# Causal attention with the rotary partner rows fetched by transfers, a new order of the shared expert's batches, and 71 routed blocks

## The chip, the cores and the metric

One NeuronCore of one Trainium2 chip runs the whole program as one launch. The metric is the device time in microseconds (us); lower is better. PE is the tensor engine, DVE the vector engine, ACT the scalar engine, POOL the GpSimd engine, and SP the engine that only issues transfers (ACT and POOL issue some too).

## What is computed

x has shape (8, 512, 512). A gated layer of biased cross-attention comes first, then a gated block of causal attention with rotary embeddings and a mixture of experts:

```python
x = x + tanh(g_xattn[0]) * xattn(layernorm(x), ctx, ctx, ...)      # 16 heads of 32
x = x + tanh(g_ffn[0])   * ffn(layernorm(x), ...)
# ffn(h):
def _rope(xh):                       # rotates pairs of the last 32 of each head's 64
    x0, x1 = xr[..., 0], xr[..., 1]
    rot = stack([x0 * cos - x1 * sin, x0 * sin + x1 * cos], -1)
h = h + attention(rmsnorm(h, w_ln1))         # causal, 16 heads, keys from a latent of 64
xn = rmsnorm(h, w_ln2)
logits = xn @ Wgate + expert_bias            # 8 experts, each token takes 2
h = h + shared_expert(xn) + sum over its 2 experts e of p_e * expert_e(xn)
# an expert: (silu(xn @ Wg) * (xn @ Wu)) @ Wd, inner size 256
```

There are 4096 tokens, so 8192 pairs of a token and an expert.

## The kernel before

The program has three passes, each written out as one instruction list per engine. **Pass A** (to about 900 us of the span) is the cross-attention, batch by batch. **Pass B** (`pass_b`, L790, about 850 to 1765 us) is the causal attention. **Pass C** (`pass_c`) is the rest: the shared expert and the routing of all 8 batches (about 1767 to 1992 us), then the routed experts (to the end).

In pass B each batch is 64 steps. In a step PE makes one unit of scores (L1537 to L1539), which ACT turns into exponentials (L1284), and one unit for the row maxima (L1554, L1555), which DVE reduces (L1412). Score and maximum units have two PSUM banks each: PE may not write a bank before its reader of two units ago is done. Between the units PE does "jobs" of the next batch: HT transposes the input, LAT makes the key latent, QN, QR the plain and the rotary rows of the queries for each of 4 head groups, K and V keys and values, SP the spread of the sums, O the output product, M a transpose of maxima. A table `plan` (L898) gives each job its steps and its bank; the reader of a job's bank comes one step after the job's last step (`evict`, on ACT at L1222 and on DVE at L1335), and `free` (L1437) makes PE wait for it before the bank's next job.

The rotary part goes in "turns": one for the keys ("k", from LAT) and one for each head group (from QR), 5 in a batch, 40 in all. For a turn DVE multiplies the PSUM rows by the cosines into `rc` (L1349); ACT and DVE split them into two float16 parts `qu_hi`, `qu_lo` (L1248, L1361); PE multiplies both by a matrix `swp` that swaps the rows in pairs with a sign (jobs KSW and QSW, L1480 and L1481); DVE multiplies the result by the sines into `rs` (L1368). Two steps after the job POOL adds `rs` to `rc` (L1174), then ACT and POOL split the sum into `qr_hi`, `qr_lo` (L1260, L1177), and SP stores these rows and loads them back into the stacks that the units read.

In pass C the shared expert works on batch b while batch b + 1 is made ready. PE does `up` (48 products of 512 columns), `turn` (transposes of batch b + 1), `route` (48 products of 8 columns), `down` (24 of 512) and `rank`. ACT has in this order for batch b: `normalise(b+1)`, `squash(b,0)` (L1996), two `high(b+1)` (L1961), `hidden_high(b,0)` (L2002), two `scale_gate`, `squash(b,1)`, two more `high`, `hidden_high(b,1)`, two `scale_gate`, `square(b+2)` (L1969), `exponential(b+1)`, `weights(b+1)`. `square(b+2)` reads the batch that SP loads into `z[:, (b+2) % 3]`, the buffer of batch b - 1. SP issues that load (L1786) once POOL's `add_to_output(b-1)` (L1849), which adds 1 MB of finished rows to the output in HBM, has landed; and that waits for DVE's `finish_rows` of batch b - 1 (L2260). POOL's list of batch b is `add_to_output(b-1)`, the record copies, the scatters of records into a table (L1872, 8 indirect transfers per batch), two `low_part` (L1853) and `rms(b+2)` (L1843, L1845).

The routed experts take `NB` = 72 blocks of 128 rows in a pipeline (`over`, L1765: 4 blocks written out, 16 turns of a loop of 4, and the last 4 with the drain written out).

```python
                sp.wait_ge(out_stored[b % 3], 16 * (b // 3))     # load_z, b >= 3
            act.wait_ge(z_loaded[b % 3], ...)                    # square
            act.wait_ge(up_done, 4 * b + 2 * i + 1)              # squash
```

## Time and profile before

| | |
|---|---|
| device time, 3 runs | median 2361.26 us (2359.19 to 2361.65) |
| the profiled execution's own time | 2359.61 us |
| its span in the trace | 2357.6 us |
| mean granted clock of PE | 0.963 |
| PE busy | 2130.3 us, 90% of the span |
| DVE, ACT, POOL busy | 64%, 50%, 58% |

The span is what the engines' records cover; the device time lies 2.0 us above it. Busy PE is not PE at its peak, since products overlap. A row of the timeline has the start in us, the duration in us, the engine, the line, the operation, out<-in, the shapes, how many were merged, and in brackets the engine's idle time before it and what ended it. "SPq" and "ACTq" are transfers as their engine's sequencer issues them. The clock column is the granted clock of PE as a share of 2.4 GHz; 0.50 is 1.2 GHz.

### The profile page before, as it was taken

The page shows a single profiled execution, that of the slowest core. Times are in us where ns is not written, and L with a number is a line of the kernel's source. Part 1 is how long each engine was busy: PE and PEld are TensorE (multiplying, and loading weights), DVE is VectorE, ACT ScalarE, POOL GpSimd, SP SyncE. Part 2 cuts the span into 40 slices and gives each one's busy share as a digit, 9 for nine tenths or more (in the row PEclk, how much of TensorE's full clock was granted, in tenths as well). Part 3 has the DMA queues.
Part 4 walks back from the last instruction along what each step waited for, and adds up shares of the span by engine and source line. Part 5 has one row for each costly group of instructions (what it writes and reads, how often), then busy time and mean ns, then how long its engine had stood idle before and what let it go on. Part 6 is the DMA issues. An engine that isn't in the chain of part 4 may idle for free. (4 is left out here: it accounts for less than half of the span.)

```text
span 2357.6 us, 43584 instructions
## 1 busy us (share of the span) xinstructions
PE 2130.3 (90%) x12672; PEld 972.2 (41%) x12673; DVE 1505.5 (64%) x4218; ACT 1177.9 (50%) x2316; POOL 1364.2 (58%) x1452
## 2 busy tenths in 40 slices
PE   3899999999999968899999999999976787999997
PEld 1333333333333313444444444444433343455554
DVE  3688888888888873656656656565535587344443
ACT  3355555555555543354545445454436473455553
POOL 3267767767767764265656565565451664455554
PEclk7999999999999978999999999999997898999999
DMA  5413323232332233453434435353314675666665
GB/s 172 156 56 107 95 90 108 77 113 70 107 104 76 85 101 94 139 151 95 141 119 134 129 96 161 89 155 120 102 50 118 132 179 106 110 112 113 115 108 88
DMA packets 222851, 263.78 MB, mean 112 GB/s; under 512 B 39192, under 2 KB 165004, under 8 KB 222388
## 3 DMA queue, kind: packets, MB, share of 16 engines
q1 hardware_dynamic: 197612, 212.79, 30.2%
q0 software_dynamic: 22976, 48.38, 11.9%
q8 instruction: 92, 1.51, 0.3%
q14 instruction: 99, 0.81, 0.1%
q10 hardware_dynamic: 2072, 0.28, 0.1%
HBM read 162.12 MB, written 86.80 MB: 106 GB/s over the span
## 5 line engine op out<-in xcount | busy, mean ns | idle before, releaser
L501 ACT ACTIVATE a_pt<-a_bank 128x512 f32<-128x512 f32 x512 | 305.6, 597 | 371.5 <-DVE a_bank L608 368.3
L1412 DVE CUSTOM_DVE_ANT_0 b_bank<-b_bank,b_tri 128x256 f32<-128x256 f32 (+3 forms) x512 | 253.6, 497 | 302.9 <-PE b_bank L1555 298.6
L619 DVE CUSTOM_DVE_ANT_0 a_bank<-a_bank,a_strip 128x512 f32<-128x512 f32 x512 | 353.1, 690 | 4.9 <-PE a_bank L762 4.3
L411 POOL TENSOR_TENSOR a_acc<-a_acc,a_pt 128x512 f32<-128x512 f32 x256 | 317.4, 1270 | 16.2 <-ACT a_pt L501 15.7
L1193 POOL TENSOR_TENSOR b_acc<-b_acc,b_pt 128x256 f32<-128x256 f32 (+2 forms) x384 | 270.9, 725 | 90.6 <-ACT b_pt L1284 71.3
L608 DVE TENSOR_TENSOR a_bank<-a_bank,a_band 128x256 f32<-128x256 f32 (+1 forms) x512 | 205.6, 402 | 129.6 <-PE a_bank L749 128.4
L1284 ACT ACTIVATE b_pt<-b_bank 128x256 f32<-128x256 f32 (+2 forms) x384 | 143.8, 383 | 190.9 <-PE b_bank L1539 181.0
L749 PE MATMUL a_bank<-a_q_stack,a_k_stack 128*128 128x512 f16 x512 | 199.3, 390 | 22.7 <-ACT a_pt L501 14.0
L762 PE MATMUL a_bank<-a_k_stack,a_q_stack 97*128 97x512 f16 x512 | 196.4, 384 | 4.6 <-DVE a_low L619 4.5
L1933 POOL DMA_INDIRECT out_dram<-c_z,c_to_row x72 | 114.1, 1585 | 138.7 <-DMA out_dram<-c_z,c_to_row 101.8
L408 POOL TENSOR_TENSOR a_acc<-a_pt 128x512 f32<-128x512 f32 x128 | 159.9, 1270 | 4.9 <-ACT a_pt L501 4.9
L1554 PE MATMUL b_bank<-b_k_stack,b_q_stack 96*128 96x256 f16 (+3 forms) x512 | 153.7, 300 | 9.3 <-DVE b_low L1412 5.6
L1537 PE MATMUL b_bank<-b_q_stack,b_k_stack 96*128 96x256 f16 (+3 forms) x512 | 155.5, 304 | 5.8 <-ACT b_pt L1284 4.7
L429 POOL TENSOR_TENSOR a_o_un<-a_o_un,a_den 128x512 f32<-128x512 f32 x32 | 40.8, 1276 | 204.4 <-DVE a_den L572 204.4
L1208 POOL TENSOR_TENSOR b_o_un<-b_o_un,b_den 128x512 f32<-128x512 f32 x32 | 40.7, 1273 | 196.4 <-DVE b_den L1378 191.0
L1539 PE MATMUL b_bank<-b_q_stack,b_k_stack 97*128 97x256 f16 (+3 forms) x512 | 153.4, 300 | 0.0
L1555 PE MATMUL b_bank<-b_k_stack,b_q_stack 96*128 96x256 f16 (+3 forms) x512 | 152.3, 298 | 0.0
L777 PE MATMUL a_bank<-a_pt,a_v 128*32 128x512 f32 x1024 | 142.3, 629 | 1.1 <-ACT a_pt L501 1.1
L1284 ACT ACTIVATE b_acc<-b_bank 128x512 f32<-128x512 f32 x128 | 76.4, 597 | 104.7 <-PE b_bank L1539 104.7
L749 PEld LDWEIGHTS a_bank<-a_q_stack,a_k_stack 128*128 128x128 f16 x512 | 49.5, 97 | 182.8 <-ACT a_pt L501 89.3
L1538 PE MATMUL b_bank<-b_hidden,b_far 128*128 128x128 bf16 x512 | 112.8, 220 | 0.0
L2313 DVE TENSOR_TENSOR c_xt_lo<-c_bank,c_xt_hi 128x512 f16<-128x512 f32 x72 | 49.7, 691 | 97.7 <-ACT c_xt_hi L2052 96.4
(346 smaller groups left out, 5432.3 us busy)
## 6 DMA issues: line engine op xcount, KB each, us to landing
b_q_stack<-qk_rows SPq DMA_DIRECT2D x192, 128.0 KB, 2.6
a_q_stack<-qk_rows SPq DMA_DIRECT2D x96, 128.0 KB
a_k_stack<-qk_rows SPq DMA_DIRECT2D x96, 128.0 KB
b_k_stack<-qk_rows SPq DMA_DIRECT2D x96, 128.0 KB, 2.6
a_sums<-in_x SPq DMA_DIRECT2D x34, 256.0 KB, 3.1
qk_rows<-a_qk_hi SPq DMA_DIRECT2D x64, 128.0 KB, 1.7
qk_rows<-a_qk_lo SPq DMA_DIRECT2D x64, 128.0 KB, 1.8
out_dram<-a_sums SPq DMA_DIRECT2D x32, 256.0 KB, 2.0
```

The source lines that it names most:

```text
L408: nc.gpsimd.tensor_tensor(acc[:, hh, :], pt[:, (n - HG) % SLOTS, :], mine, ALU.add).then_inc(pooled, 1)
L411: nc.gpsimd.tensor_tensor(acc[:, hh, :], acc[:, hh, :], mine, ALU.add).then_inc(pooled, 1)
L501: nc.scalar.activation(pt[:, n % SLOTS, :], st_bank[n % 2][:], ACT.Exp).then_inc(exped, 1)
L608: nc.vector.tensor_tensor(st_bank[n % 2][:, c0:c1], st_bank[n % 2][:, c0:c1], band[:, h, at:at + c1 - c0], ALU.add).then_inc(biased, 1)
L619: nc.vector.tensor_tensor_reduce(out=max_bank[step % 2][:], in0=max_bank[step % 2][:], in1=strip[:, g * HG + hh, at:at + S], scale=-1.0, s ...
L749: mm(st_bank[n % 2][:], k_stack[:, h, j * P:(j + 1) * P], q_stack[:, h, :], start=True, stop=True).then_inc(scored, 1)
L762: mm(max_bank[step % 2][:], q_stack[0:MASK + 1, h, i * P:(i + 1) * P], k_stack[0:MASK + 1, h, :], start=True, stop=True).then_inc(maxed, 1)
L1193: nc.gpsimd.tensor_tensor(sums_of, sums_of, probs(n), ALU.add).then_inc(pooled, 1)
L1284: nc.scalar.activation(probs(n), st_bank[n % 2][:, 0:w], ACT.Exp).then_inc(exped, 1)
L1412: nc.vector.tensor_tensor_reduce(out=max_bank[step % 2][:, 0:w], in0=max_bank[step % 2][:, 0:w], in1=tri[:, at:at + w], scale=-1.0, scalar ...
L1537: mm(o, k_stack[0][0:LOW, h, j * P:(j + 1) * P], q_stack[0][0:LOW, h, j * P:], start=True, stop=False)
L1554: mm(o, q_stack[0][0:LOW, h, c], k_stack[0][0:LOW, h, 0:w], start=True, stop=False)
```

## The change

Pass B: the jobs KSW and QSW, `swp` and the float16 parts of the unrotated rows are gone. ACT copies the whole float32 rows to `qu` (for the keys a further copy of 32 rows) and issues two transfers from SBUF to SBUF for each turn, one for the even and one for the odd rows, into `rs`. DVE multiplies `rs` by the sines in place, one step ahead of POOL's sum (`times_sine`); its `qu_lo` operation is gone. The signs went into the table of sines, and the turns keep their steps. Pass C: the shared expert's lists have a new order on every engine, `down` is cut in halves, records have three buffers in place of two and are scattered up to a batch later. `NB` is 71, with 15 turns of the loop and the last 7 blocks with the drain written out.

```diff
-NB = 2 * TT + E
+NB = 2 * TT + E - 1
...
-        turn_step = {r: pieces[(KSW, 0) if r == "k" else (QSW, r)][0] + 2 for r in turns["steady"]}
+        turn_step = {G3: 12, "k": 28, 0: 37, 1: 48, 2: 60}
...
+            def swap_pairs(kind, b, r, begin, end):
+                done = turns_upto(kind, b, r) - 1
+                if done:
+                    act.wait_ge(rot_sum, done)
+                for i in range(2):
+                    act.dma_start(rs[begin + i:end:2, :], qu[begin + 1 - i:end:2, :]).then_inc(swapped, 16)
...
+                if m == QR:
+                    act.wait_ge(hi_done, upto(kind, b, job, is_split))
+                    swap_pairs(kind, b, n, 0, P)
...
+            def times_sine(kind, b, r):
...
+                dve.wait_ge(swapped, 32 * turns_upto(kind, b, r))
+                nc.vector.tensor_tensor(rs[part, :], rs[part, :], rot[part, table, :], ALU.mult).then_inc(rot_sin, 1)
...
-                elif m in (KSW, QSW):
-                    src_job, hi, lo = ((LAT, 0), lat_hi, lat_lo) if m == KSW else ((QR, n), qu_hi, qu_lo)
-                    pe.wait_ge(left_dve, upto(kind, b, src_job, by_dve))
-                    pe.nop(nofuse=True)
-                    mm(o[:], swp[:], hi[:], start=True, stop=False)
-                    last = mm(o[:], swp[:], lo[:], start=False, stop=True)
...
                 if b > 1:
-                    scatter(b, (0,))
+                    scatter_some(b, 2)
                 low_part(b, 0)
-                if b == 1:
-                    scatter(0, (0, 1))
-                elif b:
-                    scatter(b, (1, 2))
-                low_part(b, 1)
-                if b == 1:
-                    scatter(0, (2, 3))
-                elif b:
-                    scatter(b, (3,))
+                if b > 1:
+                    scatter_some(b, 1)
                 if b + 2 < B:
                     rms(b + 2)
-                if b == 1:
-                    scatter(1, range(NT))
+                low_part(b, 1)
+                if b:
+                    scatter_some(b, 2 if b > 1 else NT)
...
                 squash(b, 0)
                 if more:
                     high(b + 1, 0)
                     high(b + 1, 1)
+                    scale_gate(b + 1, range(0, 2))
+                    high(b + 1, 2)
+                    high(b + 1, 3)
                 hidden_high(b, 0)
-                if more:
-                    scale_gate(b + 1, range(0, 2))
+                if b + 2 < B:
+                    square(b + 2)
                 squash(b, 1)
                 if more:
-                    high(b + 1, 2)
-                    high(b + 1, 3)
+                    scale_gate(b + 1, range(2, 4))
                 hidden_high(b, 1)
-                if more:
-                    scale_gate(b + 1, range(2, 4))
                 if b + 2 < B:
-                    square(b + 2)
+                    normalise(b + 2)
...
-            def down(b, t):
-                pe.wait_ge(h_lo_done, NI * b + NI)
+            def down(b, t, halves):
...
-                for t in range(NT):
-                    down(b, t)
+                for t in range(NT - 1):
+                    down(b, t, (0,))
+                for t in range(NT - 1):
+                    down(b, t, (1,))
+                down(b, NT - 1, (0, 1))
```

PE's list of a batch becomes: up, turns 0 and 1, up, turns 2 and 3, up, up, route, the halves of down. DVE's becomes: shares and places, low 0 and 1, activate 0, low 2 and 3, the up weights, activate 1, choose, the down weights, finish_rows; in the last batch `lay_blocks` comes after activate 0 and no longer right ahead of finish_rows.

**ACT in pass C**, the middle of batch 3. `c_th` is `squash`, `c_xt_hi` is `high`, `c_h_hi` is `hidden_high`, `c_xn,c_squares` is `square`. Before:

```order
1565 L1996 ACTIVATE c_th<-c_bank 128x512 [waits c_half_done,c_up_done]
1566 L1961 ACTIVATE c_xt_hi<-c_bank 128x4x128 [waits c_logits_done,c_up_done,c_turned] x2
1567 L2002 ACTIVATE c_h_hi<-c_hid 128x512 [waits c_downed,c_hidden]
1568 L1979 ACTIVATE c_z<-c_z,c_gate 128x512 [waits c_xn_ready]
1569 L1979 ACTIVATE c_z<-c_z,c_gate 128x512
1570 L1996 ACTIVATE c_th<-c_bank 128x512 [waits c_half_done,c_up_done]
1571 L1961 ACTIVATE c_xt_hi<-c_bank 128x4x128 [waits c_logits_done,c_up_done,c_turned] x2
1572 L2002 ACTIVATE c_h_hi<-c_hid 128x512 [waits c_downed,c_hidden]
1573 L1979 ACTIVATE c_z<-c_z,c_gate 128x512 [waits c_xn_ready]
1574 L1979 ACTIVATE c_z<-c_z,c_gate 128x512
1575 L1969 ACTIVATE c_xn,c_squares<-c_z 128x512 [waits c_turned,c_z_loaded1]
1576 L1969 ACTIVATE c_xn,c_squares<-c_z 128x512 x3
```

Of the change, the same stretch:

```order
1671 L2026 ACTIVATE c_th<-c_bank 128x512 [waits c_half_done,c_up_done]
1672 L1991 ACTIVATE c_xt_hi<-c_bank 128x4x128 [waits c_logits_done,c_up_done,c_turned] x2
1673 L2009 ACTIVATE c_z<-c_z,c_gate 128x512 [waits c_xn_ready]
1674 L2009 ACTIVATE c_z<-c_z,c_gate 128x512
1675 L1991 ACTIVATE c_xt_hi<-c_bank 128x4x128 [waits c_logits_done,c_up_done,c_turned] x2
1676 L2032 ACTIVATE c_h_hi<-c_hid 128x512 [waits c_downed,c_hidden]
1677 L1999 ACTIVATE c_xn,c_squares<-c_z 128x512 [waits c_turned,c_z_loaded2]
1678 L1999 ACTIVATE c_xn,c_squares<-c_z 128x512 x3
1679 L2026 ACTIVATE c_th<-c_bank 128x512 [waits c_half_done,c_up_done]
```

The squares of batch b + 2, which wait for its load, stood behind everything that ACT does for batch b; now the second `c_th` of batch b stands behind them.

**POOL in pass C**, one batch. `table` are the scatters, `c_h_lo` is `low_part`, `c_mean` and `c_rstd` are `rms(b+2)`. Before:

```order
765 L1849 DMA out_dram<-c_z 128x4x512 [waits c_out_done]
766 L1859 COPY c_record<-c_tok 128x8x2 [waits a_o_hi_done]
767 L1861 COPY c_record<-c_rstd 128x8
768 L1872 DMA table<-c_record,c_place_i 33792x4 [waits c_recorded,c_weighed]
769 L1872 DMA table<-c_record,c_place_i 33792x4
770 L1853 TENSOR_TENSOR c_h_lo<-c_hid,c_h_hi 128x512 [waits c_h_hi_done]
771 L1872 DMA table<-c_record,c_place_i 33792x4 [waits c_recorded,c_weighed]
772 L1872 DMA table<-c_record,c_place_i 33792x4 x3
773 L1853 TENSOR_TENSOR c_h_lo<-c_hid,c_h_hi 128x512 [waits c_h_hi_done]
774 L1872 DMA table<-c_record,c_place_i 33792x4 [waits c_recorded,c_weighed]
775 L1872 DMA table<-c_record,c_place_i 33792x4
776 L1843 TENSOR_SCALAR c_mean<-c_squares 128x4 [waits c_squared]
```

Of the change:

```order
773 L1877 DMA out_dram<-c_z 128x4x512 [waits c_out_done]
774 L1887 COPY c_record<-c_tok 128x8x2 [waits a_summed]
775 L1889 COPY c_record<-c_rstd 128x8
776 L1900 DMA table<-c_record,c_place_i 33792x4 x4
777 L1881 TENSOR_TENSOR c_h_lo<-c_hid,c_h_hi 128x512 [waits c_h_hi_done]
778 L1900 DMA table<-c_record,c_place_i 33792x4 [waits a_normed,a_o_hi_done]
779 L1900 DMA table<-c_record,c_place_i 33792x4
780 L1871 TENSOR_SCALAR c_mean<-c_squares 128x4 [waits c_squared]
781 L1873 TENSOR_TENSOR c_rstd<-c_mean,c_power 128x4 [waits c_rstd_done]
782 L1881 TENSOR_TENSOR c_h_lo<-c_hid,c_h_hi 128x512 [waits c_h_hi_done]
783 L1900 DMA table<-c_record,c_place_i 33792x4 x4
784 L1877 DMA out_dram<-c_z 128x4x512 [waits c_out_done]
```

The scatters are now 10 in a batch, and `c_mean`, which needs the squares, moved ahead of the second `c_h_lo`.

**ACT in pass B**, a turn of head group 0 of the change (before, `b_qu_hi` stood in the place of `b_qu`, with no transfer behind it):

```order
925 L1305 ACTIVATE b_pt<-b_bank 128x256 [waits b_pooled,b_scored]
926 L1263 ACTIVATE b_qu<-b_bank 128x512 [waits b_swapped,b_job_done]
927 L1232 DMA b_rs<-b_qu 64x512 [waits b_rot_sum,b_hi_done]
928 L1232 DMA b_rs<-b_qu 64x512
929 L1305 ACTIVATE b_pt<-b_bank 128x256 [waits b_pooled,b_scored]
```

The next exponential stands behind both transfers.

## Rows read from the trace of the kernel before

**Rows 1.** Windows: window, length, busy us (instructions) of each engine, clock, DMA share, GB/s.
```profile
1040.00:1680.00 640.00, 625.04 (x4361) 309.94 (x4360) 387.04 (x1130) 322.54 (x698) 365.35 (x477) 1.00 0.42 125
...
1792.00:1992.00 200.00, 165.62 (x1104) 84.06 (x1104) 143.69 (x447) 112.87 (x214) 106.47 (x115) 0.90 0.62 128
```
**Rows 2.** Timeline of PE: a swap job's first product, and the scores behind it.
```profile
1377.59 0.38 PE L1480 MATMUL b_bank<-b_qu_hi,b_swp 128*128 128x512 f16 x1
...
1378.02 0.33 PE L1537 MATMUL b_bank<-b_q_stack,b_k_stack 96*128 96x384 f16 x1
```
**Rows 3.** Who waited for whom, 980 to 1700 us: us in total, times, longest.
```profile
PE b_bank L1453 <- DVE b_qu_lo L1361: 8.9, 7, 1.3
```
**Rows 4.** Transfers of pass B: count, KB each, us to landing; and one that ACT issues.
```profile
b_k_stack<-b_kr_hi SPq DMA_DIRECT2D x56, 128.0 KB, 2.4
...
1316.39 0.52 ACTq L1288 DMA_DIRECT2D b_q_stack<-b_m_row  x1
```
**Rows 5.** Timeline at the turns of head groups 1 and 2, ACT, PE and DVE.
```profile
1332.43 0.60 ACT L1248 ACTIVATE b_qu_hi<-b_bank 128x512 f16<-128x512 f32 x1 [0.38 <-PE b_bank L1455]
...
1336.90 0.69 DVE L1368 TENSOR_TENSOR b_rs<-b_bank,b_rot 128x512 f32<-128x512 f32 x1
...
1350.44 0.60 ACT L1284 ACTIVATE b_acc<-b_bank 128x512 f32<-128x512 f32 x1
...
1351.93 0.32 PE L1537 MATMUL b_bank<-b_q_stack,b_k_stack 96*128 96x384 f16 x1
```
**Rows 6.** Chain of waits, routed blocks: start, us, transposes of two blocks four apart.
```profile
2102.39 0.65 PE c_bank L2451 x4
...
2120.82 0.66 PE c_bank L2451 x4
```
**Rows 7.** Timeline of DVE: last finish_rows of batches 0, 5 and 7.
```profile
1818.53 0.75 DVE L2260 SCALAR_TENSOR_TENSOR c_z<-c_bank,c_gate,c_z 128x512 f32<-128x512 f32 x1 [0.54 <-PE c_bank L2416]
...
1946.34 0.75 DVE L2260 SCALAR_TENSOR_TENSOR c_z<-c_bank,c_gate,c_z 128x512 f32<-128x512 f32 x1 [0.54 <-PE c_bank L2416]
...
1989.46 2.73 DVE L2260 SCALAR_TENSOR_TENSOR c_z<-c_bank,c_gate,c_z 128x512 f32<-128x512 f32 x4 [0.23 <-DVE c_block_i L2238]
```
**Rows 8.** Timeline of POOL and SP: add_to_output of batches 0, 1, 3, and the load behind each.
```profile
1819.59 1.42 POOL L1849 DMA_DIRECT2D out_dram<-c_z  x1 [5.53 <-DVE c_z L2260]
...
1834.48 0.37 SPq L1786 DMA_DIRECT2D c_z<-z_all  x1
...
1857.68 1.45 POOL L1849 DMA_DIRECT2D out_dram<-c_z  x1
...
1869.14 0.37 SPq L1786 DMA_DIRECT2D c_z<-z_all  x1
...
1902.92 1.44 POOL L1849 DMA_DIRECT2D out_dram<-c_z  x1 [1.38 <-DVE c_z L2260]
...
1912.35 0.37 SPq L1786 DMA_DIRECT2D c_z<-z_all  x1
```
**Rows 9.** Timeline of ACT: first square behind two loads; squash(4,1).
```profile
1843.39 0.63 ACT L1969 ACTIVATE c_xn<-c_z 128x512 f32<-128x512 f32 x1 [9.63 <-DMA c_z<-z_all]
...
1910.71 0.60 ACT L1996 ACTIVATE c_th<-c_bank 128x512 f32<-128x512 f32 x1
...
1919.11 0.63 ACT L1969 ACTIVATE c_xn<-c_z 128x512 f32<-128x512 f32 x1 [2.40 <-DMA c_z<-z_all]
```
**Rows 10.** Timeline: activate on DVE to low_part on POOL; group of the scatters.
```profile
1885.25 0.69 DVE L2247 SCALAR_TENSOR_TENSOR c_hid<-c_th,c_bank 128x512 f32<-128x512 f32 x1 [2.40 <-ACT c_th L1996]
...
1887.41 1.16 POOL L1853 TENSOR_TENSOR c_h_lo<-c_hid,c_h_hi 128x512 f16<-128x512 f32 x1 [1.93 <-ACT c_h_hi L2002]
...
L1872 POOL DMA_INDIRECT table<-c_record,c_place_i x64 | 68.8, 1075 | 30.9 <-issue 15.7 <-DVE c_record L2199 9.2 <-DMA table<-c_blank 5.2
```
**Rows 11.** PE behind a long wait, and the window of the 4 us from there.
```profile
1839.18 0.61 PE L2414 MATMUL c_bank<-c_d_hi,c_h_hi 128*128 128x512 f16 x1 [5.59 <-POOL c_h_lo L1853]
...
1839.00:1843.00 4.00, 3.82 (x10) 1.34 (x11) 0.75 (x1) 0.00 (x0) 3.04 (x4) 0.50 1.17 335
```

More of the change, by code:

```diff
@@ L917, in pass_b @@
         names = [j for j, _, _ in plan]
-        ahead = [j for j in names if j[0] in (HT, LAT, KSW, V) or j[0] in (K, QN, QR, QSW) and j[1] < G3]
+        ahead = [j for j in names if j[0] in (HT, LAT, V) or j[0] in (K, QN, QR) and j[1] < G3]
         behind = [j for j in names if j[0] == O or j == (SP, G3)]
@@ L1089, in body @@
                     weights(2)
-                    for dst, src in ((idn[:], ident), (swp[:], swap), (rot[:], cos_sin), (tri[:], causal), (later_keys[:], later)):
+                    for dst, src in ((idn[:], ident), (rot[:], cos_sin), (tri[:], causal), (later_keys[:], later)):
                         sp.dma_start(dst, src).then_inc(const_loaded, 16)
@@ L1169, in rotate @@
             def rotate(kind, b, r, low_part):
-                job, hi, lo = ((KSW, 0), kr_hi, kr_lo) if r == "k" else ((QSW, r), qr_hi, qr_lo)
+                hi, lo = (kr_hi, kr_lo) if r == "k" else (qr_hi, qr_lo)
                 if not low_part:
-                    pool.wait_ge(left_dve, upto(kind, b, job, by_dve))
+                    pool.wait_ge(rot_sin, turns_upto(kind, b, r))
                     nc.gpsimd.tensor_tensor(rc[:], rc[:], rs[:], ALU.add).then_inc(rot_sum, 1)
@@ L1238, in evict @@
                 elif m == LAT:
+                    swap_done(kind, b, "k")
+                    nc.scalar.activation(qu[KR, :], src[KR], ACT.Copy, scale=scale).then_inc(kr_raw, 1)
                     out, src = lat_hi[0:R + DH, :], src[0:R + DH]
@@ L1421, in body @@
                         evict(kind, b, job)
+                    for r in turns[kind]:
+                        if turn_step[r] - 1 == step:
+                            times_sine(kind, b, r)
                     yield
@@ L1745, in pass_c @@
             sem(n) for n in ("logits_done", "routed", "expd", "chosen_set", "ranked", "placed", "weighed", "recorded"))
-        scattered = [sem(f"scattered{i}") for i in range(2)]
+        scattered = [sem(f"scattered{i}") for i in range(3)]
         ranks_read, spare_found, blank_set, blanked, table_ready = (
@@ L1771, in over @@
                     call(Count(i, 4 + u, 4))
-            for j in range(NB - 4, NB + 1):
+            for j in range(NB - 4 - NB % 4, NB + 1):
                 call(Count(0, j, 4))
@@ L2016, in _ @@
                 high(0, t)
+            square(1)
             scale_gate(0, range(NT))
-            square(1)
+            normalise(1)
             exponential(0)
@@ L2284, in _ @@
                     find_spare()
-                activate(b, 0)
-                if not more:
-                    lay_starts()
-                    low_part(0)
                 if more:
@@ L2291, in _ @@
                     low(b + 1, 1)
+                else:
+                    lay_starts()
+                activate(b, 0)
+                if more:
+                    low(b + 1, 2)
+                    low(b + 1, 3)
+                else:
+                    low_part(0)
+                    lay_blocks()
                 if b:
@@ L2297, in _ @@
                 if more:
-                    low(b + 1, 2)
-                    low(b + 1, 3)
+                    choose(b + 1)
                 if b:
                     down_weights(b)
-                if more:
-                    choose(b + 1)
-                else:
-                    lay_blocks()
                 for t in range(NT):
@@ L2412, in down @@
                 c = slice(t * P, (t + 1) * P)
-                for i in range(NI):
+                for i in halves:
+                    pe.wait_ge(h_lo_done, NI * b + i + 1)
                     mm(tile_bank[t][:], h_hi[:, i, c], d_hi[:, i, :], start=(i == 0), stop=False)
@@ L2416, in down @@
                     last = mm(tile_bank[t][:], h_lo[:, i, c], d_hi[:, i, :], start=False, stop=(i == NI - 1))
-                last.then_inc(downed, 1)
+                if NI - 1 in halves:
+                    last.then_inc(downed, 1)
             pe.wait_ge(const_loaded, 16 * 11)
@@ L2434, in _ @@
                     turn(b + 1, 1)
+                up(b, 0, 1)
+                if more:
+                    turn(b + 1, 2)
+                    turn(b + 1, 3)
                 up(b, 1, 0)
```

142 lines of the change are left out of this document (75 added, 67 removed).

## The prediction

> **What bounds the kernel now.** I read the windows first, stage by stage, since the page's 90% of PE is a mean over stages. In pass B, PE is busy for 625 of 640 us at the full 2.4 GHz (clock 1.00) and no other engine for more than 387 [rows 1]: there a product removed from PE is time gained, unless its place is taken by a wait. In the shared expert's stage PE is busy for only 166 of 200 us at a mean clock of 0.90, with the DMA engines busy for 62% [rows 1]: there the order of waits decides, so I followed single batches on the timelines. The routed blocks are one pipeline with a steady period, read off the chain of waits [rows 6]. The profiled execution took 2359.61 us, 1.65 below the median of 2361.26; I sum against the first and add the 1.65 at the end. About 0.2%, 4.7 us, is what a measurement can tell from no change.
>
> **Pass B, removed.** A swap job is two products, and the scores behind it start 0.43 us after its first [rows 2]. Of 40 jobs four belong to the first batch's preparation, where PE isn't the bound; 36 x 0.43 = 15.5 us. PE also waited 7 times, 8.9 us in all, for DVE's `qu_lo` to leave a bank [rows 3]. That operation is gone, and the bank is free as soon as ACT has copied it and DVE has multiplied it by the cosines; an operation less of this kind is worth about 0.6 us (ACT's twin of it takes 0.60 [rows 5]), 7 x 0.6 = 4.2 us. Together -19.7.
>
> **Pass B, added.** Three things take some back. (1) At the turn of head group 1 ACT itself was waiting for PE, 0.38 us, just before the copy [rows 5], so 0.3 us of the job there was cover for something else: 7 x 0.3 = +2.1. (2) ACT now issues two transfers before the next exponential, 0.52 us each by the one transfer that it issues in pass B [rows 4]. At the turn of group 2 an exponential ends at 1351.04 and PE's next scores begin at 1351.93 [rows 5], a margin of 0.9 us against 1.04 of issue; with a little jitter 0.2 to 0.5 us in each of 7 batches, +2.5. (3) The swapped rows must land before DVE's sines. At the turn of group 1 the copy ends at 1333.03, the issues end at 1334.1, and a transfer of 128 KB, the size of a turn's whole swap, lands 2.4 us after its issue in this pass [rows 4]: 1336.5, against the sines at 1336.90 [rows 5], which now come about 0.4 earlier, since DVE has one operation less. The margin is nil; I take it 0.5 us late in 7 batches, +3.5. At the other turns some 1.6 us more lie between the two. The turns keep their steps, so POOL's sum, the splits and SP's stores stay where they were; they are later only if the sines are. Pass B: -19.7 + 2.1 + 2.5 + 3.5 = **-11.6**, with ends -19.7 (all hidden) and about +5 (rival B).
>
> **Routed blocks.** Four blocks take 18.43 us [rows 6], so one fewer is -4.6. That three more of them are written out and one loop turn fewer is run moves no work of an engine; I cost it at nothing. **-4.6.**
>
> **The shared expert's stage.** Here the order counts. On ACT the four squares of batch b + 2 now stand ahead of the second `squash` of batch b. They wait for a load into the buffer of batch b - 1; the load waits until the store of that batch's rows has landed; the store waits for `finish_rows(b-1)`. Everything behind the second `squash` (activate, `hidden_high`, `low_part`, the second halves of `down`, `finish_rows(b)`) thus waits for `finish_rows(b-1)` through two 1 MB transfers, in batches 1 to 5. Before, the squares were last in ACT's list, and the wait for the load was spent after the hidden rows were on their way. The closed loop of one batch is then:
> - from `finish_rows` to the issue on POOL: 1819.59 - 1819.28 = 0.3 [rows 7, 8];
> - store to the load's issue on SP: 14.9, 11.5 and 9.4 us for batches 0, 1 and 3 [rows 8];
> - load to first square: 8.9 (1834.48 to 1843.39) and 6.8 (1912.35 to 1919.11) [rows 8, 9];
> - four squares of 0.63, then `squash`, 0.60 [rows 9]: 3.1;
> - activate to the end of `low_part`: 1885.25 to 1888.57, 3.3 [rows 10];
> - 15 products of 512 columns and the last `finish_rows`. PE has idled for some 10 us by then (a loop of 30.1 against 166/8 = 20.7 of PE work a batch [rows 1]); behind a wait of 5.59 us it ran at clock 0.50 for the next 4 us, 10 products at about 0.4 [rows 11]. So 9 x 0.4 + 6 x 0.215 (half of a pair at full clock [rows 2]) + 0.54 + 0.75 [rows 7] = 6.2.
>
> The last three steps are 12.6. Batch 1 has the long store and load: 0.3 + 14.9 + 8.9 + 12.6 = 36.7. In batch 2, the store of batch 1 is issued behind 8 scatters of 1.075 + 0.25 us (15.7 us of issue over 64 [rows 10]), 10.6 in all, of which 6.2 lie beside `down`: 4.4 + 11.5 + 6.8 + 12.6 = 35.3. Batches 3 to 5, with the mean of 11.5 and 9.4: 0.3 + 10.4 + 6.8 + 12.6 = 30.1 each. The sum from `finish_rows(0)` to `finish_rows(5)` is 162.3 us; before it was 1947.09 - 1819.28 = 127.8 [rows 7]: **+34.5**. One row says plainly that the loop bites: `squash(4,1)` ran at 1910.71, and the batch that it would now wait for came at 1919.11 [rows 9]. The last two batches have no load ahead of them; they took 1992.19 - 1947.09 = 45.1 [rows 7] and can't be under 2 x 166/8 = 41.4 of PE work [rows 1]. PE's turns of batch b + 1 are no longer in front of `route`, and `lay_blocks` is off the end (the last `finish_rows` came 0.23 behind it [rows 7]): 41.8, **-3.3**. Batch 0 and the passage from pass B: nothing, since nothing in their path moved behind a transfer.
>
> Bounds of the loop: every store 9.4, every load 6.8 and no slow clock (15 x 0.215 + 1.3 = 4.5 for the last step) give 27.4 a batch and 31.5 in batch 2, 141.1, +13.3; every store 14.9 and load 8.9 would give about +60, and is excluded for more than a batch or two by the later rows. I take the middle rows, since batches 3 to 5 run under the same traffic as the rows they come from.
>
> **Sum:** -11.6 - 4.6 + 34.5 - 3.3 = +15.0, so 2374.6 for a profiled execution, **2376** for the median.
>
> **Rivals.** *A, the other side: the loop is short.* With stores and loads at the lower ends (+13.3) the total is -6.2: 2353.4, median **2355**. It speaks for it that a PE that waits asks for fewer weights and that records are scattered later, so that the transfers have the engines to themselves; against it, 9.4 is already the shortest store of the three shown. It decides where the five cycles average less than 127.8 + 19.5 = 147.3, 29.5 us each, instead of 32.5. 14%.
> *A2: the two transfers cost about half.* With half of the shortest rows, 9.4 and 6.8, the two take 8.1 and a loop 0.3 + 8.1 + 12.6 = 21.0 us, about PE's own 20.7 a batch and below the 25.6 of before (127.8/5), and the stage would lose nothing: -19.5, median **2342**. No row is near that. 3%. The Trainium skill, "DMA: Bandwidth & Descriptors", section "Anatomy of one DMA — SWDGE (gpsimd) path", gives a fit of 2.0 us plus bytes over 436 GB/s, which by estimate is 4.4 us for 1 MB and 8.8 for the two; by that rule the loop is harmless. The trace disagrees, by a factor of two for the store.
> *B: the swaps come late.* They share engines with SP's stores and reloads, 42% busy in this pass [rows 1], and the margin at group 1 is nil. If DVE waits at most turns, the maxima behind it come late, PE waits, and pass B ends about 5 us longer instead of 11.6 shorter: median **2393**. Against it: most turns have 1.6 us to spare. 15%. The Trainium skill, same page, "Queues, rings and completion order", has ACT's queue as one ring on each of the same 16 engines as SP's, not as engines of its own; the 42% is what this trace shows of it.
> *C: the change doesn't remove what it says.* If half of the removed pairs only filled PE's waits for exponentials, pass B gains 4 instead of 11.6: median **2384**. PE's 98% busy speaks against much of it. 13%.
>
> **Numbers.** The forecast has 55%; of it 12 lie within 4.7 us of no change (loops of 29 to 30 us). Faster: A and A2, 0.17. Same 0.12. Slower: 43 + 15 + 13, 0.71. The range from A's 2352 to B's 2393 leaves out A2, and the tails of the long loop.
>
> **What would show it.** In the profile after: on ACT, `squash` or squares in batches 1 to 5 behind a wait for the load of `c_z`, and PE idle by some 10 us ahead of the second halves of `down`, then at clock 0.50; `finish_rows(0)` to `finish_rows(5)` near 162 us; 71 blocks at 4.6. In pass B a batch about 1.6 us shorter than before, PE's wait for `qu_lo` gone, DVE waiting for `b_rs` by half a microsecond at group 1. I am wrong if the five cycles average under 29.5 us, if PE doesn't wait there at all, or if DVE waits for `b_rs` at every turn.

## The result and the profile after

The change takes 2392.05 us (median of 4 runs, 2389.51 to 2397.52) against 2360.23 us: the ratio is 1.0139, 95% interval 1.0119 to 1.0159. It is slower by 31.8 us where the forecast's sum was +15.0. The shared expert's stage lost about what was forecast; pass B, which was to give 11.6 us back, lost time as well.

The profiled execution is the slowest of the four, 2397.52 us, with a span of 2395.7 us. That is 38.1 us above the span of before, so its sums below explain some 6 us more than the medians differ by. The windows of the change, the same two stretches as in [rows 1], with the same columns:

```profile
1040.00:1680.00 640.00, 608.73 (x4235) 300.04 (x4232) 377.63 (x1090) 320.38 (x693) 371.51 (x472) 0.99 0.46 136
1792.00:1992.00 200.00, 132.62 (x958) 69.79 (x959) 111.38 (x360) 109.67 (x218) 84.49 (x94) 0.81 0.53 120
```

In pass B, PE is busy 16 us less in 640 us, and that became idle time, not a shorter pass. In the shared expert's stage it is busy 133 us in place of 166, at a lower clock.

**Pass B.** I compare the starts of PE's score units (64 in a batch). First the timeline of the kernel before, at units 0 and 36 of batch 3 and at 36 and 52 of batch 4; then the change, at units 0, 36 and 52 of batch 3 and at 36 and 52 of batch 4:

```profile
1267.94 0.38 PE L1537 MATMUL b_bank<-b_q_stack,b_k_stack 96*128 96x512 f16 x1
...
1330.97 0.33 PE L1537 MATMUL b_bank<-b_q_stack,b_k_stack 96*128 96x384 f16 x1
...
1432.39 0.33 PE L1537 MATMUL b_bank<-b_q_stack,b_k_stack 96*128 96x384 f16 x1
...
1453.34 0.32 PE L1537 MATMUL b_bank<-b_q_stack,b_k_stack 96*128 96x384 f16 x1
```
```profile
1276.73 0.38 PE L1561 MATMUL b_bank<-b_q_stack,b_k_stack 96*128 96x512 f16 x1
...
1337.88 0.33 PE L1561 MATMUL b_bank<-b_q_stack,b_k_stack 96*128 96x384 f16 x1
...
1360.81 0.34 PE L1561 MATMUL b_bank<-b_q_stack,b_k_stack 96*128 96x384 f16 x1 [0.30 <-ACT b_acc L1305]
...
1439.36 0.33 PE L1561 MATMUL b_bank<-b_q_stack,b_k_stack 96*128 96x384 f16 x1
...
1466.73 0.34 PE L1561 MATMUL b_bank<-b_q_stack,b_k_stack 96*128 96x384 f16 x1 [0.30 <-ACT b_acc L1305]
```

The delay against before is 8.79 us at unit 0 of batch 3, 6.91 at unit 36 and 8.88 at unit 52 (before: 1351.93 [rows 5]). So the removed swaps do give 1.9 us in the first 36 steps, and 16 steps later it is all gone. In batch 4 the same stretch loses 6.4 us (6.97 to 13.39), the most of any batch. What happens between is the turn of head group 1; here that of batch 4, on SP, ACT, DVE and PE:

```profile
1440.51 0.40 SPq L1125 DMA_DIRECT2D b_sums<-out_dram  x1
...
1440.82 0.60 ACT L1263 ACTIVATE b_qu<-b_bank 128x512 f32<-128x512 f32 x1 [0.38 <-PE b_bank L1485]
...
1441.44 1.13 ACTq L1232 DMA_DIRECT2D b_rs<-b_qu  x2
...
1442.04 2.27 SPq L1034 DMA_DIRECT2D qk_rows<-b_kn_hi  x1
...
1450.82 0.69 DVE L1410 TENSOR_TENSOR b_rs<-b_rs,b_rot 128x512 f32<-128x512 f32 x1 [5.26 <-DMA b_rs<-b_qu]
...
1452.24 0.39 PE L1578 MATMUL b_bank<-b_k_stack,b_q_stack 96*128 96x512 f16 x1 [3.92 <-DVE b_low L1439]
```

ACT has issued both transfers by 1442.57, and the rows are there 8.2 us later, at about 1450.8. DVE stands in front of its sines for 5.26 us, its row maxima are late, and PE, which may not write a maximum bank before they are read, waits 3.92 us. The first row is a load of 1 MB that SP issues once a batch. In all seven batches it is issued 0.1 to 2.2 us ahead of the second transfer of this turn; that second transfer lands 5.4 to 8.8 us after its issue, where the transfers of all other turns take 1.8 to 4.6 us, 2.2 in the median. The view of who waited for whom, 980 to 1700 us, shows that DVE's wait is one place in every batch (total, times, longest):

```profile
DVE b_rs L1410 <- DMA b_rs<-b_qu: 19.6, 7, 5.3
PE b_bank L1578 <- DVE b_low L1439: 11.8, 7, 3.9
PE b_bank L1561 <- ACT b_pt L1305: 9.4, 22, 0.8
PE b_bank L1483 <- DVE b_rc L1370: 5.1, 7, 1.0
```

**The shared expert's stage.** The last `finish_rows` of batches 0 to 5 and 7 on DVE:

```profile
1833.74 0.75 DVE L2289 SCALAR_TENSOR_TENSOR c_z<-c_bank,c_gate,c_z 128x512 f32<-128x512 f32 x1 [0.52 <-PE c_bank L2445]
...
1865.19 0.75 DVE L2289 SCALAR_TENSOR_TENSOR c_z<-c_bank,c_gate,c_z 128x512 f32<-128x512 f32 x1 [0.54 <-PE c_bank L2445]
...
1901.48 0.75 DVE L2289 SCALAR_TENSOR_TENSOR c_z<-c_bank,c_gate,c_z 128x512 f32<-128x512 f32 x1 [1.15 <-PE c_bank L2445]
...
1931.79 0.75 DVE L2289 SCALAR_TENSOR_TENSOR c_z<-c_bank,c_gate,c_z 128x512 f32<-128x512 f32 x1 [1.55 <-PE c_bank L2445]
...
1960.60 0.75 DVE L2289 SCALAR_TENSOR_TENSOR c_z<-c_bank,c_gate,c_z 128x512 f32<-128x512 f32 x1 [0.54 <-PE c_bank L2445]
...
1990.74 0.75 DVE L2289 SCALAR_TENSOR_TENSOR c_z<-c_bank,c_gate,c_z 128x512 f32<-128x512 f32 x1 [0.65 <-PE c_bank L2445]
...
2035.39 0.75 DVE L2289 SCALAR_TENSOR_TENSOR c_z<-c_bank,c_gate,c_z 128x512 f32<-128x512 f32 x1 [0.54 <-PE c_bank L2445]
```

The loops of batches 1 to 5 took 31.5, 36.3, 30.3, 28.8 and 30.1 us, 157.0 in all. They close as the forecast said. ACT, squares behind the load, and the tanh of batch 1 behind the first of them; then POOL and SP with the store and the load; then PE in front of the second halves of `down`, and the windows of 4 us from 1858 and 1862:

```profile
1853.96 0.63 ACT L1999 ACTIVATE c_xn<-c_z 128x512 f32<-128x512 f32 x1 [11.39 <-DMA c_z<-z_all]
...
1856.43 0.57 ACT L2026 ACTIVATE c_th<-c_bank 128x512 f32<-128x512 f32 x1
...
1889.02 0.63 ACT L1999 ACTIVATE c_xn<-c_z 128x512 f32<-128x512 f32 x1 [15.40 <-DMA c_z<-z_all]
```
```profile
1834.80 1.41 POOL L1877 DMA_DIRECT2D out_dram<-c_z  x1 [4.57 <-DVE c_z L2289]
...
1848.03 0.37 SPq L1810 DMA_DIRECT2D c_z<-z_all  x1
```
```profile
1860.48 0.58 PE L2443 MATMUL c_bank<-c_d_hi,c_h_hi 128*128 128x512 f16 x1 [10.93 <-POOL c_h_lo L1881]
...
1858.00:1862.00 4.00, 1.51 (x4) 0.58 (x5) 3.48 (x19) 3.75 (x8) 2.33 (x3) 0.50 0.00 0
1862.00:1866.00 4.00, 4.00 (x24) 1.81 (x23) 3.04 (x6) 2.12 (x4) 3.08 (x4) 0.86 0.55 134
```

Store 13.2 us, load 5.9, and PE idle for 10.93 us (8.5 to 14.5 at this place in the next four batches) before it works on at 1.2 GHz (clock 0.50), for 2.5 us and six products; from 1863.00 the clock is back. In the last batch, which has no load ahead of it, PE waited at the same place for another reason:

```profile
2030.23 0.59 PE L2443 MATMUL c_bank<-c_d_hi,c_h_hi 128*128 128x512 f16 x1 [7.47 <-DVE c_h_lo L2284]
```

There DVE makes `c_h_lo` itself, and `lay_blocks` now stands ahead of the second one.

**The routed blocks** on the chain of waits, transposes of two blocks four apart: 18.43 us, as in [rows 6].

```profile
2313.70 0.65 PE c_bank L2484 x4
...
2332.13 0.65 PE c_bank L2484 x4
```

So the 38.1 us of the two profiled executions are: 3.1 us before any changed code has run (PE's first wait for `a_pt` after 850 us, at 852.34 before and 855.43 now), +13.4 in pass B (its output products at 1757.77 and 1774.25; 4.7 of it stand ahead of batch 1 and 8.6 in batches 1 to 6), -1.3 to `finish_rows(0)`, +29.2 in the five loops, -0.5 in the last two batches and -5.8 behind them.

### The profile page after: what moved, and what is told of

Same layout as the page of the kernel before. It is cut to its first block and busy times, and to the rows that moved or that the text cites. A ratio compares the mean times of both kernels' runs of the same rounds, so it can differ in the third digit from the quotient of the medians.

```text
span 2395.7 us, 43299 instructions
## 1 busy us (share of the span) xinstructions
PE 2111.8 (88%) x12568; PEld 961.6 (40%) x12569; DVE 1492.7 (62%) x4180; ACT 1179.9 (49%) x2319; POOL 1372.0 (57%) x1450
## 5 line engine op out<-in xcount | busy, mean ns | idle before, releaser
L1192 POOL TENSOR_TENSOR b_acc<-b_acc,b_pt 128x256 f32<-128x256 f32 (+2 forms) x384 | 279.1, 746 | 85.3 <-ACT b_pt L1305 74.9
L1561 PE MATMUL b_bank<-b_q_stack,b_k_stack 96*128 96x256 f16 (+3 forms) x512 | 156.1, 305 | 14.9 <-ACT b_pt L1305 11.6
```

Of the source, the lines that this page charges most:

```text
L1192: nc.gpsimd.tensor_tensor(sums_of, sums_of, probs(n), ALU.add).then_inc(pooled, 1)
L1561: mm(o, k_stack[0][0:LOW, h, j * P:(j + 1) * P], q_stack[0][0:LOW, h, j * P:], start=True, stop=False)
```

## The experiments

The theory after the two profiles: two independent losses, DVE's wait for the swaps at head group 1, and the closed loop. The rivals: the loss in pass B is an accident of one execution; or it is ACT's issue time; or the stage is held by something else in its new order.

**1. The swaps alone.** The change with pass C and 72 blocks of before.

```diff
-NB = 2 * TT + E - 1
+NB = 2 * TT + E
...
(pass_c of the kernel before)
```

> Only the swaps by transfers; pass C and 72 blocks as before. Theory (the swaps cost time: at head group 1 DVE waits for the transfers, and what the removed products give is taken back there): 8 to 14 us slower than the kernel before, 2368 to 2374 us, with DVE's waits for b_rs at group 1 by 2 to 5 us in each batch. Rival (the forecast's sum for pass B was right, and what the profile of the change shows there came from one disturbed execution): 5 to 12 us faster than before, 2348 to 2355 us.

Measured: 2370.52 us (2370.17 to 2372.0), ratio 1.0047 [1.003, 1.0064], that is +10.9 us. The waits, 980 to 1700 us:

```profile
DVE b_rs L1410 <- DMA b_rs<-b_qu: 17.5, 7, 3.0
PE b_bank L1578 <- DVE b_low L1439: 10.3, 7, 1.9
```

The forecast's -11.6 for pass B is refuted, and the accident too. Batch 4's wait of 5.26 us is an outlier, though: here none is over 3.0.

**2. The new order alone.** The kernel before with the change's pass C, 72 blocks.

> Only the new order of the shared expert's stage; pass B and 72 blocks as before. Theory (a closed loop of store, load, squares, second tanh in batches 1 to 5): 25 to 32 us slower, 2386 to 2392 us, finish_rows(0) to finish_rows(5) at 153 to 162 us in place of 127.8. Rival (the loop is only that long because pass B ended late or the swaps disturbed something): under 10 us slower.

Measured: 2394.81 us (2393.58 to 2397.43), ratio 1.0146 [1.0129, 1.0163], +35.2 us, above what was expected. `finish_rows(0)` to `finish_rows(5)` took 158.7 us and to `finish_rows(7)` 202.9, where before has 172.9: the stage accounts for 30 of it. Another 4.9 us were there in the first steps of pass B already, whose code is that of before. PE's first score unit, where the passes hand over, came up to 6.2 us later than in the one profile of before in all twelve profiles of this section (0.05 us in experiment 10). The swaps may have a part in what follows: from the wait at 852.34 us of before to batch 1, the kernels with swaps lose a further 1.8 to 7.4 us and this one 1.5. Why wasn't tested.

**3. The squares back behind.** The change, with this on ACT, and `rms(b + 2)` behind `low_part(b, 1)` on POOL:

```diff
                 hidden_high(b, 0)
-                if b + 2 < B:
-                    square(b + 2)
                 squash(b, 1)
...
                 if b + 2 < B:
-                    normalise(b + 2)
+                    square(b + 2)
                 if more:
                     exponential(b + 1)
                 weights(b + 1)
+                if b + 2 < B:
+                    normalise(b + 2)
```

> The change with the squares of batch b + 2 back behind the second hidden_high on ACT, its normalise behind the weights, and rms back behind the second low_part on POOL; all else as in the change. Theory (only that place closes the loop): the stage falls from 157 to 120 to 130 us between the finish_rows of batches 0 and 5, so 27 to 37 us less than the change: 2355 to 2365 us. Rival (the stage is held by the halves of down or by the later scatters): still over 2380 us.

Measured: 2377.65 us (2373.16 to 2384.11), 14.4 below the change: a miss for both cases. The first loop fell from 31.5 to 19.8 us, the next ones only to 31.4, 28.0 and 26.6. PE now waited at its turns, which the new order asks for a product earlier. PE, then ACT:

```profile
1856.05 1.97 PE L2392 MATMUL c_bank<-c_idn,c_xn 128*128 128x128 f32 x8 [4.78 <-ACT c_xn L2004]
```
```profile
1849.25 0.63 ACT L1999 ACTIVATE c_xn<-c_z 128x512 f32<-128x512 f32 x1 [5.54 <-DMA c_z<-z_all]
...
1855.30 2.54 ACT L2004 ACTIVATE c_xn<-c_z,c_rstd 128x512 f32<-128x512 f32 x4
```

**4. 72 blocks.** The change with `NB = 2 * TT + E`.

> The change with 72 routed blocks. Theory: one block more costs its period, 4.6 us: 2396 to 2398 us. Rival (the block that is left out was empty and cheap, or the tail changed otherwise): the same as the change within 2 us.

Measured: 2402.38 us, but from 2396.43 to 2407.34, 10.3 above the change, where one period is 4.6. Behind `finish_rows(7)` its profiled execution has 363.5 us against 359.6, 3.9 more; the rest of its difference lies ahead of that point, in code that is the same. The runs spread too far to say more than that the block costs about its period.

**5. Head group 1 later.** Experiment 1 with one number changed:

```diff
-        turn_step = {G3: 12, "k": 28, 0: 37, 1: 48, 2: 60}
+        turn_step = {G3: 12, "k": 28, 0: 37, 1: 51, 2: 60}
```

> The swaps-only kernel with head group 1's sine, sum and split three steps later (turn_step 51 in place of 48). Theory (the sines at step 47 come before the transfers have landed, and DVE's wait takes back the gain): the waits for b_rs at group 1 go and the kernel is 7 to 12 us shorter than swaps only, 2358 to 2364 us. Rival (the loss is ACT's two issues ahead of the exponentials, or anything else but the landing): within 3 us of swaps only, 2368 to 2374 us.

Measured: 2360.02 us (median of 10, 2352.15 to 2365.36), ratio 0.9992 [0.9978, 1.0007], 10.5 below experiment 1. DVE's wait for `b_rs` and PE's for `b_low` are gone from its list of waits. Nearly all of the 10.9 us by which experiment 1 is slower than before stood at this one turn. But the kernel is now only as fast as before, not 11.6 us faster; experiment 7 shows a part of the rest.

**6. Short rows.** Experiment 1 with 16 columns of each row moved, the rest of `rs` left as it was:

```diff
-                    act.dma_start(rs[begin + i:end:2, :], qu[begin + 1 - i:end:2, :]).then_inc(swapped, 16)
+                    act.dma_start(rs[begin + i:end:2, 0:16], qu[begin + 1 - i:end:2, 0:16]).then_inc(swapped, 16)
```

> The swaps-only kernel with 16 columns of each row in the transfers in place of 512 (the rest of rs keeps old values, so this leaves most of the swap out). Issues and waits stay. If the landing is late because of the bytes and the traffic beside them, DVE's wait at group 1 goes below 1 us and the kernel is 5 to 10 us shorter than swaps only. If it is late by a fixed latency of a transfer, or if the loss is ACT's issue time, it stays within 3 us of swaps only.

Measured: 2364.5 us (median of 10, 2360.55 to 2380.6), 6.0 below experiment 1, as the first case has it; but the waits of the profiled execution contradict that case. That execution took 2369.72 us, only 0.5 less than the profiled one of experiment 1, so it doesn't show what the others gained. Transfers of experiment 1, then of this one (count, KB, us to landing), and its waits:

```profile
b_rs<-b_qu ACTq DMA_DIRECT2D x64, 128.0 KB, 2.6
```
```profile
b_rs<-b_qu ACTq DMA_DIRECT2D x64, 4.0 KB, 2.1
```
```profile
DVE b_rs L1410 <- DMA b_rs<-b_qu: 17.6, 7, 3.6
PE b_bank L1578 <- DVE b_low L1439: 9.1, 7, 2.3
```

A thirty-second of the bytes lands 0.5 us sooner in the median, and in this execution DVE waits as long as before: the swap's own bytes are not all that makes it late. With 4 KB each, the second transfer at head group 1 still lands 5.3 to 8.0 us after its issue, and at the other turns none takes over 3.3. A transfer's latency alone doesn't explain that either. What sets this turn apart is SP's traffic. The 1 MB load of `b_sums` is issued just ahead of the swap in each batch; in experiment 1, in six batches of seven, the two transfers land 0.9 to 2.0 us behind it. SP's stores of `kn` and loads of the stacks come at the same time, and its issue of `kn_hi` took 2.27 us in the change, where that of `b_qn_lo` ahead of it took 0.42. A kernel with SP's transfers moved away from the turn wasn't tried, so that they cause the delay, and the load of 1 MB above all, is argued and not shown.

**7. Transfers behind the exponential.** Experiment 5, with the swap of a query turn issued behind the next exponential on ACT.

```diff
-                if m == QR:
-                    act.wait_ge(hi_done, upto(kind, b, job, is_split))
-                    swap_pairs(kind, b, n, 0, P)
...
                         nc.scalar.activation(probs(n), st_bank[n % 2][:, 0:w], ACT.Exp).then_inc(exped, 1)
+                    for job in ended(kind, step - 1):
+                        if job[0] == QR:
+                            act.wait_ge(hi_done, upto(kind, b, job, is_split))
+                            swap_pairs(kind, b, job[1], 0, P)
```

> As the kernel with head group 1 three steps later, and the query turns' transfers are issued behind the next exponential instead of ahead of it. Theory (the two issues, 1.1 to 1.2 us on ACT, delay an exponential that PE waits for at 2 to 3 turns of a batch by 0.3 to 0.5 us): a further 4 to 8 us shorter than that kernel. Rival (the issue is hidden, or the wait only moves to the next exponential): within 2 us of it.

Measured: 2357.07 us (median of 10, 2347.66 to 2360.81), ratio 0.998 [0.9968, 0.9992], 3.0 below experiment 5. That is between the two cases; the runs of the two kernels overlap, so I count it as a small gain at most. PE's waits for exponentials didn't fall (12.6 us in 17 waits, against 11.3 in 22): the 0.46 us that unit 52 of each batch lost behind the issues are gone, but unit 58 now loses 0.85 us where it lost 0.41.

What stands there is not an issue. In the turn of head group 2, DVE multiplies by the sines while POOL adds. POOL's rows of batch 3, before; then DVE and POOL of the change:

```profile
1355.65 1.95 POOL L1193 TENSOR_TENSOR b_acc<-b_acc,b_pt 128x384 f32<-128x384 f32 x2
```
```profile
1363.37 1.29 DVE L1410 TENSOR_TENSOR b_rs<-b_rs,b_rot 128x512 f32<-128x512 f32 x1
...
1364.07 2.41 POOL L1192 TENSOR_TENSOR b_acc<-b_acc,b_pt 128x384 f32<-128x384 f32 x2
```

POOL's two additions take 0.46 us longer. Behind them come its sum `b_rc`, ACT's `qr_hi` (ACT stands idle for 1.14 us ahead of it before, for 1.55 in the change) and the exponential that PE's unit 58 waits for, 0.36 us before and 0.77 in the change. In experiment 7 the issues no longer delay PE, and this chain is all that does. No run took it away, so its worth is read from the rows only.

**8. Normalise ahead of the weights.** Experiment 3, with this on ACT:

```diff
                 if more:
                     exponential(b + 1)
+                if b + 2 < B:
+                    normalise(b + 2)
                 weights(b + 1)
-                if b + 2 < B:
-                    normalise(b + 2)
```

> As the kernel with the squares last, but normalise(b+2) stands ahead of the routed experts' weights(b+1) on ACT, not behind them. There PE waited 4.8 us in a batch for the normalised rows of its turns, which the new order asks for earlier. Theory (that turn is the new end of the store, load, squares chain, and the weights' 3.4 us stand in it): 3 us less in each of 5 or 6 batches, 2360 to 2368 us. Rival (the stage is bound by the store and the load whatever stands behind them, or by the weights themselves): within 4 us of squares last.

Measured: 2378.48 us (2374.78 to 2384.16), no gain, as the rival has it. The loops stay at 32.0, 26.5, 27.9, 26.8. POOL shows what holds them. The `finish_rows` of batch 2 ended at 1887.21 (1886.46 + 0.75); POOL:

```profile
1889.27 0.19 POOL L1871 TENSOR_SCALAR c_mean<-c_squares 128x4 f32<-128x4 f32 x1 [6.38 <-ACT c_xn L1999]
...
1894.72 0.96 POOL L1900 DMA_INDIRECT table<-c_record,c_place_i  x1 [0.30 <-issue]
...
1895.67 1.47 POOL L1877 DMA_DIRECT2D out_dram<-c_z  x1
```

The store is issued 8.5 us late: it stands behind `rms(b + 2)`, which waits for the squares of the load of one batch earlier, and behind four scatters. It is a second closed loop: store, load, squares, `rms`, scatters, store.

**9. Scatters ahead of rms.** Experiment 8, with this on POOL:

```diff
                 low_part(b, 1)
+                if b:
+                    scatter_some(b, 2 if b > 1 else NT)
                 if b + 2 < B:
                     rms(b + 2)
-                if b:
-                    scatter_some(b, 2 if b > 1 else NT)
```

> As the kernel with the squares last and normalise ahead of the weights, but on POOL the scatters of a batch stand ahead of rms(b+2), not behind it. Theory (a second closed loop: rms waits for the squares, and add_to_output of the batch stood behind rms and four more scatters of 1.3 us, 8.5 us after finish_rows): the loop of 26.7 us a batch loses those 5.2 us, down to 22 to 23 in five batches, so 12 to 22 us less, 2357 to 2366 us. Rival (store and load themselves became slower with the new order, and nothing on POOL matters): within 4 us of 2378.

Measured: 2371.46 us (2370.8 to 2376.68), 7.0 below experiment 8, where 12 to 22 were expected: a miss for both cases. The store now goes out at 1885.75, 2.1 us after `finish_rows`. But the loops stayed at 29.4, 26.7, 26.0, 27.0: now `rms` is late behind the scatters, and ACT's and PE's rows show the rest, in that order:

```profile
1885.81 2.56 ACT L2004 ACTIVATE c_xn<-c_z,c_rstd 128x512 f32<-128x512 f32 x4 [5.04 <-POOL c_rstd L1873]
```
```profile
1893.60 1.64 PE L2392 MATMUL c_bank<-c_idn,c_xn 128*128 128x128 f32 x8 [3.15 <-DVE c_xt_lo L2120]
```

**10. Both repairs.** Experiment 9 with the swaps of experiment 7:

```diff
-        turn_step = {G3: 12, "k": 28, 0: 37, 1: 48, 2: 60}
+        turn_step = {G3: 12, "k": 28, 0: 37, 1: 51, 2: 60}
...
(the swaps behind the exponential, as in 7)
```

> The kernel before this one together with head group 1 three steps later and the swaps behind the exponential, 71 blocks. The swaps' gains and the order's are in different stages and should add: the swaps-late kernel was 13.5 us below swaps only, so this is 11 to 16 us below the kernel with the scatters ahead of rms: about 2345 to 2352 us if that one comes at 2360.

Measured: 2357.32 us (median of 10, 2354.5 to 2366.54), ratio 0.9998 [0.9983, 1.0014]. It is 14.1 below experiment 9, in the 11 to 16 expected: the two parts add.

**11. Old order, 71 blocks, late swaps.** The change with the swaps of experiment 7 and every engine's list of the shared expert's stage as before (the records keep their three buffers); on PE, for one:

```diff
                 up(b, 0, 0)
                 if b == 0:
                     rank(0)
+                up(b, 0, 1)
                 if more:
                     turn(b + 1, 0)
                     turn(b + 1, 1)
-                up(b, 0, 1)
+                up(b, 1, 0)
+                up(b, 1, 1)
                 if more:
                     turn(b + 1, 2)
                     turn(b + 1, 3)
-                up(b, 1, 0)
-                up(b, 1, 1)
```

> The shared expert's stage in its old order, 71 blocks with the tail written out, head group 1 three steps later and the swaps behind the exponential. Sum of what the parts showed: 2357.1 of the swaps-late kernel less 4.6 to 5.8 for a block, 2351 to 2353 us. Rival (the old order was best and the 71st block cost more than its period, as the 10 us between 71 and 72 blocks of the change hints): 2345 to 2348 us.

Measured: 2349.60 us (median of 6, 2347.98 to 2355.53), ratio 0.9959 [0.9945, 0.9973]: faster than both kernels, and 7.5 below experiment 7, between the two cases. One block is 4.6 of it; the profiled execution, 2354.29 us, doesn't show what the rest is.

**12. Batch 1's scatters spread.** In experiment 11 the store of batch 1 went out at 1854.98, 7.6 us after `finish_rows(1)`, behind eight scatters in a row.

```diff
                 if b > 1:
-                    scatter_some(b, 1)
+                    scatter_some(b, 2)
...
                 if b + 2 < B:
                     rms(b + 2)
-                if b == 1:
-                    scatter_some(1, NT)
```

> As the kernel with the old order and 71 blocks, but batch 1's eight scatters don't stand in a block ahead of add_to_output(1); from batch 2 on ten scatters go out in a batch, as in the change. In the kernel before this one add_to_output(1) was issued 7.6 us after finish_rows(1), and batch 2 took 30.5 us. Theory: batch 2 falls to about 25 us and later batches, with two scatters more each, grow by under 1: 3 to 6 us less, 2344 to 2347 us. Rival (the scatters only move, into the wait of the store in batches 2 to 6, where each then delays low_part): within 1.5 us, 2348 to 2351.

Measured: 2348.26 us (median of 6, 2342.56 to 2350.82), ratio 0.9953 [0.9939, 0.9967]. The wait went (the store is issued at 1843.11), and batch 2 fell from 30.5 to 22.7 us in the profiles; between the batches 0 and 7 the stage takes 169.7 us in place of 173.1. The medians differ by 1.3 us, within the spread, as the rival has it, though the mechanism was the theory's: batch 2 gained and later batches gave some of it back. It isn't shown to be faster than experiment 11. It is the fastest kernel here, some 11 us below the kernel before by its ratio.

## Why the prediction was wrong

The direction and the loop of the shared expert's stage were right; the size was not, 31.8 us in place of 15.0. The measured 2392.05 us lies next to rival B's 2393, but that is luck: B had most turns late, pass B 5 us longer and the loops at +34.5; pass B lost more than that, at one turn of a batch, and the loops cost 29.2.

- **"Pass B: -19.7 + 2.1 + 2.5 + 3.5 = -11.6" is the step that failed.** Alone it costs +10.9 (experiment 1). The term that was mis-sized most is (3), "I take it 0.5 us late in 7 batches": the rows were 1.9 to 5.3 us late in the change, 19.6 in all, and 2 to 3 in experiment 1, 17.5 in all. I took the 2.4 us of a transfer's median landing, and allowed nothing for the transfers that run beside it. The 1 MB load of `b_sums` at this turn stood in the trace of the kernel before as well (issued at 1331.65, 0.8 us ahead of the copy of [rows 5]), and the prediction has no term for it. I also had the size wrong: 128 KB is each of the two transfers, the whole swap is 256 KB. And five short steps lie between the copy and the sines. The price of a late sine was under-sized too: DVE's maxima stand behind it, so PE waited for most of it, 11.8 us. That is rival B's mechanism, at one turn in a batch and not at most of them; experiment 5 takes that one turn away and 10.5 us with it.
- **The rest of pass B** fell short as well, or experiment 5 would be 11.6 us faster than before and not 0.6. The removal shows on the starts of the units as 1.9 us up to unit 36 and 0.4 from unit 52 to 57, 2.3 us a batch where 19.7 in 7 batches are 2.8; PE's wait for a bank at `qu_lo`, 8.9 us, shrank only to 5.1, at `b_rc`. Then 0.4 to 0.85 us are lost again at unit 58 of each batch (experiment 7), a chain through POOL that I had put at nothing. And the preparation and batch 0, at nothing in the forecast too, were 1.8 to 7.4 us slower in every profile of a kernel with swaps than in the one of before (1.5 us in experiment 2, without swaps). From batch 1 to batch 7 experiments 7, 11 and 12 gain 5.0, 7.6 and 8.2 us. So a part of the removed work seems to have filled waits, as rival C has it, though not half of it.
- **Term (2), ACT's issues,** was forecast at 2.5 us. Two issues take 1.1 to 1.2 us, and a unit behind them starts 0.3 to 0.5 us later at two turns of a batch. Moving them gave 3.0 us (experiment 7).
- **The closed loop was right.** Forecast 36.7, 35.3 and three of 30.1, 162.3 in all; measured 31.5, 36.3, 30.3, 28.8, 30.1, 157.0. PE's wait ahead of the second halves of batch 1 is 10.93 us where some 10 were forecast. Behind it clock 0.50 held for six products, 2.5 us, where the forecast had nine in 4 us. The loop of batch 1 was shorter mainly because the load took 5.9 us and not 8.9, and the store 13.2 and not 14.9.
- **Rivals A and A2 fell:** no store of the change took under 9.4 us and the average loop was 31.4, not under 29.5. The Trainium skill's fit ("DMA: Bandwidth & Descriptors", "Anatomy of one DMA — SWDGE (gpsimd) path") gives 4.4 us by estimate for 1 MB on POOL's path; the stores, which POOL issues, took 9.6 to 13.2 us, so this trace disagrees. The fit is for that path, so the 8.8 us for the pair stretched it to SP's load too; store and load took 19.2 us in batch 1.
- **"41.8, -3.3" for the last two batches** was wrong by 2.8 us. `lay_blocks` left the place ahead of `finish_rows` and went ahead of `c_h_lo`, where PE waits for it, 7.47 us. I had followed who no longer waited and not who now does.
- **The block** is worth about its period of 4.6: the time behind `finish_rows(7)` fell by 5.8 against before, and by 3.9 against the change with 72 blocks (experiment 4).
- **What I had not seen in the stage** is that the place of the squares isn't all: with them back, the new order still held a second loop through POOL (experiments 8 and 9), and PE's earlier turns a third wait (experiment 3). From `finish_rows(0)` to `finish_rows(7)` the five profiles with the order of before have 170.7 to 173.1 us, the seven with a new order on ACT, DVE and PE 181 to 203.

## What to carry to other kernels

When a product is replaced by a transfer, the transfer's median landing is no budget: look at what other queues issue in the same microseconds, a large load above all, take the steps at their shortest, and ask what stands behind the consumer on its engine. Three steps more of distance were worth 10.5 us here. An engine that isn't the bound can still delay the one that is, through a chain of waits. In a pipeline over batches, write down for each in-order engine what stands behind a wait for a load, and follow it to the store that frees the buffer: a loop that closes within one batch sets the period, and taking one item out of it may only show the next one.

## What the runs showed of the hardware

Transfers from SBUF to SBUF, issued in pairs, land 2.1 us after their issue with 4 KB each and 2.6 us with 128 KB each (medians of pass B, experiments 6 and 1): 32 times the bytes for 0.5 us. With a 1 MB load issued by SP at most 2.2 us earlier, the second of a pair landed after 5.4 to 8.8 us in the change, and with 4 KB still after 5.3 to 8.0 us.

DVE's multiply by the sines read PSUM before and took 0.69 us [rows 5], also beside POOL. In place in SBUF the same shape averages 0.89 us in the change: 0.69 us where POOL did nothing, up to 1.29 us where POOL added. At head group 2 it took 1.29 us in every batch, and POOL's addition beside it 1.45 us in place of 1.0. No multiply of this shape took over 0.70 us without POOL at work beside it; a run that separates the two wasn't made. This shape alone, 980 to 1700 us:

```profile
L1410 DVE TENSOR_TENSOR b_rs<-b_rs,b_rot 128x512 f32<-128x512 f32 x29 | 25.8, 888 | 19.6 <-DMA b_rs<-b_qu 19.6
```
